# First MoE of a four-block transformer kernel: expert tiles with the output matmuls one tile later, residual ahead of bias on VectorE, rstd ahead of the second bias on GpSimd, and 39 tiles instead of 40

## The reference, cut to what matters

```python
xr = x.reshape(-1, d)                      # 4096 tokens
logits = xr @ moe_gate_w + moe_gate_b
top_v, top_i = jax.lax.top_k(logits, 2)
chosen = jnp.max(top_i, axis=-1)           # one of 8 experts for each token
...
def expert(W1, B1, G, Bt, W2, B2, rsc):    # W1 256x512, W2 512x256
    hh = xr @ W1 + B1
    hh = jax.nn.gelu(_ln(hh, G, Bt), approximate=False)
    return (hh @ W2 + B2) * rsc + xr
```

## Time and profile before

| | us |
|---|---|
| median of 3 runs | 2383.2 (2380.38 to 2383.29) |
| profiled execution, its own time | 2397.18 |
| its span | 2395.5 |
| TensorE busy / VectorE / ScalarE / GpSimd | 76% / 63% / 41% / 25% of the span |
| expert tiles: first T to the end of the last fin | 1488.34 to 1679.36, 191.0 |

### The profile page before, as it was taken

The page is one execution under the profiler, slowest core; times in us unless marked ns, Lnnn a source line. Parts: engine busy times, 40 slices in busy tenths (PEclk is TensorE's granted clock), DMA queues, the critical chain, the costliest instruction groups (busy, mean ns, idle before and its releaser), DMA issues. The chain is left out here.

```text
span 2395.5 us, 30402 instructions
## 1 busy us (share of the span) xinstructions
PE 1824.8 (76%) x8414; PEld 835.8 (35%) x8415; DVE 1505.9 (63%) x2941; ACT 972.5 (41%) x1284; POOL 601.4 (25%) x573
## 2 busy tenths in 40 slices
PE   4799795899999999999996843998037986113997
PEld 2355451222222222222224631555023553002564
DVE  5688354888787887888842441555656895692121
ACT  1355361366565665666673311343214553000110
POOL 2344245100000000000002434332723442047233
PEclk8999896799999999999997865999569998556999
DMA  4000286111121111112004023111210004202342
GB/s 118 0 0 0 90 283 199 32 33 33 33 63 33 33 32 34 32 41 55 1 1 155 0 97 127 55 55 48 75 33 0 0 0 141 79 1 60 81 97 35
DMA packets 112376, 137.14 MB, mean 57 GB/s; under 512 B 14208, under 2 KB 88448, under 8 KB 112000
## 3 DMA queue, kind: packets, MB, share of 16 engines
q1 hardware_dynamic: 97280, 113.59, 16.1%
q0 software_dynamic: 9216, 16.79, 3.1%
q10 hardware_dynamic: 5760, 5.25, 0.7%
HBM read 78.44 MB, written 57.15 MB: 57 GB/s over the span
## 5 line engine op out<-in xcount | busy, mean ns | idle before, releaser
L873 DVE TENSOR_REDUCE sa_mpart<-sa_a 128x1 f32<-128x512 f32 x1024 | 653.8, 686 | 141.9 <-PE sa_a L959 135.0
L941 ACT ACTIVATE sa_e<-sa_b 128x1024 f32<-128x1024 f32 x512 | 499.5, 1022 | 314.4 <-PE sa_b L986 314.3
L959 PE MATMUL sa_a<-sa_k,sa_q 96*128 96x512 bf16 x1024 | 386.3, 404 | 60.4 <-DMA sa_k<-k_parts 26.7
L986 PE MATMUL sa_b<-sa_q,sa_k 98*128 98x512 bf16 x1024 | 311.1, 386 | 10.0 <-issue 7.6
L996 PE MATMUL sa_ops<-sa_e,sa_v 128*17 128x512 f32 x2048 | 272.3, 602 | 0.0
L959 PEld LDWEIGHTS sa_a<-sa_k,sa_q 96*128 96x128 bf16 x1024 | 87.6, 97 | 451.1 <-DVE sa_mpart L873 408.3
L1098 POOL TENSOR_TENSOR ao_var<-ao_mv,x_eps_pow 128x4 f32<-128x4 f32 x8 | 1.6, 201 | 910.1 <-DVE ao_mv L1197 910.1
L300 POOL TENSOR_TENSOR xa_prob<-xa_prob,xa_rden 128x1024 f32<-128x1024 f32 x64 | 121.6, 1902 | 191.8 <-DVE xa_rden L247 191.8
L421 PE MATMUL xa_score<-xa_kblk,xa_qst 128*128 (+1 forms) x256 | 133.9, 628 | 20.3 <-ACT xa_qst L343 19.2
L986 PEld LDWEIGHTS sa_b<-sa_q,sa_k 98*128 98x128 bf16 x1024 | 96.9, 99 | 107.5 <-issue 39.3
L235 DVE TENSOR_REDUCE xa_mx<-xa_score 128x16 f32<-128x1024 f32 x64 | 77.9, 1217 | 54.3 <-PE xa_score L425 27.9
(11 more groups left out here) (308 smaller groups left out, 2793.3 us busy)
## 6 DMA issues: line engine op xcount, KB each, us to landing
sa_q<-q_parts SPq DMA_DIRECT2D x16, 768.0 KB, 6.3
sa_k<-k_parts SPq DMA_DIRECT2D x16, 768.0 KB, 9.3
tc_w<-in_L_ffn_W SPq DMA_DIRECT2D x24, 512.0 KB, 6.3
k_parts<-sp_kpart SPq DMA_DIRECT2D x16, 384.0 KB, 3.2
q_parts<-sp_qpart SPq DMA_DIRECT2D x16, 384.0 KB, 2.9
expert_in<-ao_zero SPq DMA_DIRECT2D x1, 5120.0 KB, 23.2
expert_out<-ex_xb ACTq DMA_DIRECT2D x40, 128.0 KB, 1.7
v_groups<-sp_vt SPq DMA_DIRECT2D x8, 544.0 KB, 3.6
```

The source lines that it names most:

```text
L873: nc.vector.tensor_reduce(mpart[par][:, head, rest // 2, rest % 2:rest % 2 + 1], aps[k % 2][:], axis=X, op=ALU.max).then_inc(max_done, 1)
L941: nc.scalar.activation(ex[kt % 2][p][:], bps[p][:], ACT.Exp, scale=SCALE).then_inc(exp_done, 1)
L959: nc.tensor.matmul(aps[k % 2][:], qs[s][0:KROWS, head, q0:q0 + P], ks[s][0:KROWS, head, (rest % 2) * CW:(rest % 2 + 1) * CW], start=True, ...
L986: last = nc.tensor.matmul(bps[p][:, head % 2], ks[s][:, head, kt * P:(kt + 1) * P], qs[s][:, head, qc * CW:(qc + 1) * CW], start=True, sto ...
```

## The change

On TensorE, body k now does Y(k - 1) between T(k) and H(k + 3), where it did H(k + 3) and then Y(k). The last Y comes after the bodies. On VectorE fin(k - 1) comes ahead of add(k + 3), no longer behind it. On ScalarE the store of tile k - 2 is issued at the head of body k, not at its end. On GpSimd body k makes rstd(k + 3) first and then b2(k + 1). SP's own body is unchanged. MT is 39, and `turns` has three straight bodies at the end in place of four, none of which works ahead.

```diff
--- before.py
+++ after.py
@@ -1035,7 +1035,7 @@
                 transpose_out(UNITS)
 
 E8 = 8
-MT = TILES + E8
+MT = TILES + E8 - 1
 F1 = 512
 FK = F1 // P
 
@@ -1434,11 +1434,11 @@
 
             for j in range(U):
                 body(j, 0, j, True)
-            with eng.Fori(1, MT // U - 1) as i:
+            with eng.Fori(1, MT // U) as i:
                 for j in range(U):
                     body(i * U + j, i, j, True)
-            for j in range(U):
-                body(MT - U + j, MT // U - 1, j, j + AHEAD < U)
+            for k in range(MT // U * U, MT):
+                body(k, k // U, k % U, False)
 
         def expert(eng, k):
             return eng.value_load(tile_expert[0:1, ds(k, 1)], min_val=0, max_val=E8 - 1)
@@ -1461,7 +1461,7 @@
                     load(k, k)
                 turns(sp, body)
                 for i in range(U):
-                    sp.wait_ge(y_stored[i], 16 * (MT // U))
+                    sp.wait_ge(y_stored[i], 16 * len(range(i, MT, U)))
 
             @block.tensor
             def _(pe):
@@ -1493,8 +1493,12 @@
                     for f in range(FK):
                         last = nc.tensor.transpose(tps[j % 2][:, f * P:(f + 1) * P], hb[j][:, f * P:(f + 1) * P], ident[:])
                     last.then_inc(hT_psum, 1)
+                    if later(k, 1):
+                        outputs(k - 1, (j - 1) % U)
                     if ahead:
                         hidden(k + AHEAD, (j + AHEAD) % U)
+
+                def outputs(k, j):
                     e = expert(pe, k)
                     pe.wait_ge(hT_ready, k + 1)
                     pe.wait_ge(y_ready, k + 1)
@@ -1508,6 +1512,7 @@
                     transpose_x(k, 0, k)
                     hidden(k, k)
                 turns(pe, body)
+                outputs(MT - 1, (MT - 1) % U)
 
             @block.scalar
             def _(act):
@@ -1534,17 +1539,17 @@
                     act.dma_start(gathered_out[ds(P * k, P), :], xb[j][:]).then_inc(y_stored[j], 16)
 
                 def body(k, turn, j, ahead):
+                    if later(k, 2):
+                        store(k - 2, (j - 2) % U)
                     if ahead:
                         evacuate_xT(k + AHEAD, (j + AHEAD) % U)
                     gelu(k, j)
-                    if later(k, 2):
-                        store(k - 2, (j - 2) % U)
 
                 for k in range(AHEAD):
                     evacuate_xT(k, k)
                 act.wait_ge(ew["b_loaded"], ew["b_count"])
                 turns(act, body)
-                for k in (MT - 2, MT - 1):
+                for k in range(MT - 2, MT):
                     store(k, k % U)
 
             @block.vector
@@ -1571,10 +1576,10 @@
                                                    in1=xb[j][:], op0=ALU.mult, op1=ALU.add).then_inc(y_ready, 1)
 
                 def body(k, turn, j, ahead):
+                    if later(k, 1):
+                        finish(k - 1, (j - 1) % U)
                     if ahead:
                         add_b1(k + AHEAD, (j + AHEAD) % U, expert(dve, k + AHEAD))
-                    if later(k, 1):
-                        finish(k - 1, (j - 1) % U)
                     if ahead:
                         apply_norm(k + AHEAD, (j + AHEAD) % U)
 
@@ -1607,10 +1612,10 @@
                                             ALU.add).then_inc(xb_ready, 1)
 
                 def body(k, turn, j, ahead):
+                    if ahead:
+                        make_rstd(k + AHEAD, (j + AHEAD) % U)
                     if not isinstance(k, int) or k + 1 < MT:
                         add_b2(k + 1, turn + (j + 1) // U, (j + 1) % U)
-                    if ahead:
-                        make_rstd(k + AHEAD, (j + AHEAD) % U)
 
                 pool.wait_ge(ew["b2_scaled"], 1)
                 pool.wait_ge(y_ready, 2)
```

## The result

The changed kernel takes 2425.42 us (2421.34 to 2427.21, 4 runs) where the kernel before takes 2381.79 (2374.35 to 2383.29, 4 runs); the ratio is 1.018, 95% interval 1.0163 to 1.0197. The prediction said slower, 2396 us, and 2387 to 2404: the direction was right, the size far too small.

What follows compares the result with a forecast made beforehand. A ring through SP's load, 10.86 us per two bodies, was to bound the kernel: 19.1 us lost, 8.1 gained at the end, 2.0 for late reads, so 13 more than 2383.2: 2396 us, range 2387 to 2404.

Steps and rivals of the forecast that it cites:

- the ring through the load: From H(k+3) over add, rstd, b2 and SP's load to X(k+5) and H(k+5): 10.86 us for two bodies.
- late reads: TensorE's sequencer reads Y's expert number only after the load landed, in eight bodies: 2.0 us, between 0 and 4.8.
- The granted clock stays at 1.00: Sign expected in the new profile: TensorE's granted clock in the changed stage remains 1.00.
- TensorE's clock falls in the waits: Rival: one pair of bodies in five at 1.2 GHz, 13 us more, 2409; chance 0.07.
- Elsewhere it rides on the first weight load, and the sequencer has gone on: Outside eight bodies, X's wait for the load does not hold TensorE's sequencer, so no cost was added there.
- VectorE's and ScalarE's edits costed at nothing: VectorE's 2.75 us a body was taken to fit in TensorE's 4.27; the sum has no term for these edits.
- the tail's gain: Behind T(36) to the stage's end: 9.7 us in place of 17.8, by the missing tile and overlap, 8.1 gained.
- The faster rival: The load is in time and TensorE's order sets bodies of 4.27 us: 28 us less, 2355; chance 0.08.

Runs made afterwards that it cites:

- e1: The changed kernel with GpSimd's b2(k+1) ahead of rstd(k+3) again, as before; 2371.12 us, ratio 0.9952.
- e2: The kernel before with GpSimd's order alone changed: rstd(k+3), then b2(k+1); 2383.20 us, ratio 1.0003.
- e7: The kernel before with only TensorE's new order and 39 tiles; GpSimd, VectorE and ScalarE in the old order; 2348.91 us, ratio 0.9870.
- e8: The changed kernel with VectorE and ScalarE in the order of before, GpSimd's b2 still late; 2418.16 us, ratio 1.0160.
- e9: e3 with the read of Y's expert number moved ahead of X on TensorE; ratio 1.0060 to the kernel before.
- e3: The changed kernel with two filler matmuls, read by nobody, behind H in each body; 2407.54 us, ratio 1.0113.

## Why the prediction was right and wrong

**The bound, and the ring through the load: right.** It closes only with TensorE's order and the late b2 together (e1, e2, e7, e8), and its length, with the clock up and no late reads, is 10.88 us (e9) against 10.86 summed. That it fits to 0.02 is in part luck. In one round of e9 (1592.77 to 1603.68, 10.91) the way from the load's issue to X takes 2.30 where 2.04 was summed, but X to H takes 2.43 for 2.55 and H to add 2.04 for 2.13.

**"The granted clock stays at 1.00": wrong, this is the largest error.** The prediction left the clock out of its sum and gave "TensorE's clock falls in the waits" 0.07, because a stretch with 80% busy had kept 0.99. What it looked at was the busy share. It expected waits of 0.8 to 1.5 us in nearly every body; every second X waits instead, 2.0 to 2.9 us, and the clock went to 0.90. The price is 19.0 us of stage time by e3, 16.9 by the changed kernel's own rounds. The 13 us that the rival was priced at came near this by luck: it took three rounds in sixteen at 4.4 us each, and it was eleven at some 1.5.

Behind 12 of the 17 waits the clock fell to the lower level and came back. Behind five, of 2.3 to 2.5 us, it stayed up, so the length of the wait doesn't decide alone, and no run shows what does. The rule of the Trainium skill that was cited there ("TensorE: Matmul & The Clock Gate", "Part 1: The HAM clock gate") says that the clock is halved after idle time and comes back with sustained work; the trace agrees in that the clock falls in this stage only behind waits, and is 0.99 in e3, where they are 0.3 to 0.8 us but for the first.

The clock and the ring feed each other. Behind a round at full clock the next wait is 2.0 to 2.3 us, behind a slow one 2.3 to 2.5 (the first 2.04). From T to T it takes 6.4 to 6.9 us to a body whose X waits; from there to the next it takes 4.6 to 4.7 with the clock up and 5.9 to 6.4 with it down. The prediction had 5.1 and 5.7.

**"Elsewhere it rides on the first weight load, and the sequencer has gone on": wrong.** The prediction let the expert's number be read late in eight bodies, for 2 us in all. It is read late in every body that waits for its load. The X at 1575.34 had its wait on the weight load, and TensorE's sequencer (PEldq) reads the number for the Y behind it only then. Its one read between 1573.2 and 1576.4:

```profile
L1444 PEldq TENSOR_LOAD <-sm_tile_expert x1: 308/308/308, 1575.6 to 1575.6; - x1
```

In seven of nine such bodies T to Y is 0.80 or 0.81 us (0.70 and 0.96 in the other two), where the prediction took 0.5. In the eight whose wait stands on the sequencer it is 0.92 to 0.97, so late by 0.42 to 0.47, where 0.35 was estimated. Both the count and the size were too small: late reads are worth 9.0 us (e9 against e3) and not 2.

**VectorE's and ScalarE's edits costed at nothing: wrong.** The prediction named fin's move and never asked what fin had covered: the 0.93 us in which GpSimd makes rstd. In the changed kernel add comes 2.43 us behind H in some bodies (1571.19 to 1573.62) in place of 2.04. And the store at the head of ScalarE's body holds gelu back at the end. The last bodies of the changed kernel:

```profile
1713.68 0.60 PE L1494 MATMUL ex_tps<-x_ident,ex_hb 128*128 128x128 f32 x4
...
1717.89 0.81 ACT L1533 ACTIVATE ex_hT<-ex_tps,sm_bt,sm_g 128x128 f32<-128x128 f32 x2 [3.44 <-DVE ex_xb L1575]
...
1719.53 5.40 PE L1506 MATMUL ex_yps<-ew_w,ex_hT 128*128 x16 [2.52 <-ACT ex_hT L1533]
...
1725.07 0.48 DVE L1575 SCALAR_TENSOR_TENSOR ex_xb<-ex_yps,sm_rs,ex_xb 128x256 f32<-128x256 f32 x1 [1.50 <-PE ex_yps L1506]
```

gelu(37) starts 4.2 us behind its T, as the store ahead of it waits for a fin that stands behind norm. From T(36) to the end it takes 14.0 us, not the 9.7 predicted, so the tail's gain was 3.8 and not 8.1. Not all of this is the two edits: the last two Y take 5.40 us at the lower clock, where they take 3.71 in e3 and in e8. The same stretch is 11.1 us in e3, which has both edits and its clock up, and 10.4 in e8, which has neither.

**The faster rival (28 us less if the load were in time): its price was nearly right.** e7, which opens the ring, is 32 us faster; a body is 4.11 and not 4.27, since T to Y needs 0.44 and Y to H 1.73.

The stage adds up as follows: 191.0 before; e9, the ring at full clock with early reads, 207.3, where the prediction had 202 without late reads; e3, with late reads, 216.3; the changed kernel, at its own clock, 235.3. Of e9's 5 us over the prediction 2.7 lie ahead of T(2), 1.4 behind T(36) and 1.2 between. Ahead of T(2) the prediction let add(3) follow H(3) by 2.13 us; in the changed kernel it takes 3.59 (1491.01 to 1494.60), as norm(2) stands before it on VectorE. The rest was not taken apart: e9's fillers and VectorE's and ScalarE's edits are in it.

## What to carry to other kernels

When an order is changed, look at what each moved instruction stood between: fin filled the time in which another engine made a number, and b2, which nobody waits for directly, was what released a buffer and so started a load. Sum such rings link by link; here the sum was right to 1% at full clock with early reads. Then ask what the waits do to TensorE's clock and to the reads that the sequencers do only after a wait, since these two cost some 28 us here (19.0 and 9.0), more than the 16.3 by which e9's stage is longer than the one before.

## What was not expected of the hardware

In the changed kernel, where every second X waits 2.0 to 2.9 us, the clock granted over the stretch was 0.90; with two filler matmuls a body it was 0.99, and these 72 added matmuls made the kernel 18 us faster. A wait that rides on a weight load also holds up what the sequencer does further behind it: Y's expert is read after the load has landed, not during the wait, until the read stands ahead of X in the program (T to Y 0.81 in the changed kernel against 0.44 us in e9).
